# The inputs of the delta rule: one convolution, one projection and the sums of squares at other places in their queues

## What is computed

```python
q = silu(short_conv(hidden_states @ Wq, conv_q))      # 4 taps along the tokens
k = silu(short_conv(hidden_states @ Wk, conv_k))
v = silu(short_conv(hidden_states @ Wv, conv_v))
mix_inp = silu(short_conv(hidden_states @ Wmix, conv_mix))
q, k = silu(q), silu(k)
beta = sigmoid(hidden_states @ Wb)
gamma = sigmoid(hidden_states @ Wdec)
# delta_rule_chunkwise: q and k by their l2 norms (sums of squares by head of 64 channels),
#   attn = where(strict_lower, -(k_beta @ k^T), 0) in chunks of 32
# ema_rule: s = gamma * s + (1 - gamma) * v, one step per token
```

## Time and profile before

| | |
|---|---|
| time, median of 3 runs | 1435.75 us (1435.06 to 1437.74) |
| time of the profiled execution | 1436.34 us |
| its span in the trace | 1434.6 us |
| busy: PE | 1277.0 us (89%) |
| busy: DVE | 820.7 us (57%) |
| busy: ACT | 463.3 us (32%) |
| busy: POOL | 496.5 us (35%) |

### The profile page before, as it was taken

The page is one execution under the profiler, slowest core; times in us unless marked ns, Lnnn a source line. Parts: engine busy times, 40 slices in busy tenths (PEclk is TensorE's granted clock), DMA queues, the critical chain, the costliest instruction groups (busy, mean ns, idle before and its releaser), DMA issues. The chain is left out here.

```text
span 1434.6 us, 36334 instructions
## 1 busy us (share of the span) xinstructions
PE 1277.0 (89%) x12853; PEld 951.4 (66%) x12854; DVE 820.7 (57%) x1882; ACT 463.3 (32%) x1085; POOL 496.5 (35%) x709
## 2 busy tenths in 40 slices
PE   7999999899999999838888887298999999889997
PEld 5888888767776777614554555287888888746565
DVE  6788889533222222248888877457566666435443
ACT  1211222132222222226767774011222222123332
POOL 4344666415411111065666432223343434210000
PEclk9999999889999999968888997558999999779999
DMA  9999910113311211122444434612643334000001
GB/s 309 349 370 340 328 49 31 38 48 109 113 59 60 64 59 59 48 73 95 138 122 119 114 107 136 129 50 74 117 115 89 94 94 147 2 0 30 29 22 37
DMA packets 219962, 156.60 MB, mean 109 GB/s; under 512 B 111744, under 2 KB 201344, under 8 KB 219840
## 3 DMA queue, kind: packets, MB, share of 16 engines
q1 hardware_dynamic: 204288, 129.11, 30.7%
q0 software_dynamic: 9312, 25.44, 5.4%
q10 hardware_dynamic: 6240, 0.39, 0.3%
HBM read 64.47 MB, written 90.44 MB: 108 GB/s over the span
## 5 line engine op out<-in xcount | busy, mean ns | idle before, releaser
L945 PE MATMUL ps_sc<-w,a_qeo 128*128 x568 | 183.1, 466 | 0.0
L753 DVE TENSOR_TENSOR a_stm<-a_vpad,ps_sc 128x352 f32<-128x352 f32 x71 | 37.0, 521 | 177.2 <-ACT a_vpad L517 177.2
L945 PEld LDWEIGHTS ps_sc<-w,a_qeo 128*128 128x128 f32 x568 | 104.0, 193 | 46.5 <-issue 2.5
L423 POOL DMA_DIRECT2D x_slots<-a_stm x66 | 36.4, 551 | 226.1 <-issue 226.1
L1585 PE MATMUL d_pp<-d_xT,d_w_p 128*128 128x512 f32 x192 | 112.1, 732 | 1.1 <-ACT d_xT L1320 1.1
L1477 DVE SCALAR_TENSOR_TENSOR d_cout<-d_cin,d_taps,d_cout 128x512 f32<-128x512 f32 x144 | 106.1, 747 | 6.1 <-ACT d_cout L1338 2.7
L915 PE MATMUL ps_kv<-w,a_stm 128*128 x426 | 105.7, 384 | 1.2 <-DVE a_stm L746 1.1
L915 PEld LDWEIGHTS ps_kv<-w,a_stm 128*128 128x128 f32 x426 | 79.2, 190 | 30.1 <-issue 12.5
L2328 PE MATMUL g_pp<-g_xT,g_w_g 128*128 128x512 f32 x192 | 90.8, 613 | 8.3 <-ACT g_xT L2219 8.3
L1253 POOL DMA_INDIRECT got<-x_slots,d_idx x64 | 75.5, 1180 | 18.7 <-issue 16.1
L517 ACT ACTIVATE a_vpad<-ps_sc 128x352 f32<-128x352 f32 x71 | 33.0, 464 | 140.0 <-PE ps_sc L945 140.0
(11 more groups left out here) (273 smaller groups left out, 2834.4 us busy)
## 6 DMA issues: line engine op xcount, KB each, us to landing
x_slots<-a_zeros SPq DMA_DIRECT2D x32, 1024.0 KB, 11.0
rec<-d_kve SPq DMA_DIRECT2D x32, 384.0 KB, 2.9
u_kve<-rec SPq DMA_DIRECT2D x32, 384.0 KB, 3.9
a_qeo<-x_slots SPq DMA_DIRECT2D x71, 128.0 KB, 2.0
x_slots<-a_stm POOLq DMA_DIRECT2D x66, 128.0 KB, 2.1
rec<-d_act_out SPq DMA_DIRECT2D x32, 256.0 KB, 3.7
u_qkT<-rec SPq DMA_DIRECT2D x32, 256.0 KB, 3.5
w<-in_w SPq DMA_DIRECT2D x4, 1408.0 KB, 14.0
```

The lines of the kernel that those rows point to most:

```text
L753: dve.tensor_tensor(e_h[:, q, 0:HID], e_gate[:, q, :], ps_3[q], ALU.mult).then_inc(h_out, 1)
L945: mm = pe.matmul(ps, e_xT[:, q, k, :], w13[:, s, k, bass.ds(e_hidden, 1), :], start=(k == 0), stop=(k == KD - 1))
```

## The change

Three pieces change their places; the same instructions are executed.

On DVE, conv(2), the convolution of the first k block, stands ahead of the wait for `dec`, where it stood behind the scans. On PE, tokens(0) goes behind use(2). And the sums of squares, one piece behind use(7), are made in three: of the first tile of 128 tokens ahead of use(6), of the second ahead of use(7), of the last two where they stood. The first part waits for all the squares, as the whole did.

```diff
                 if here:
+                    conv(2)
+                if here:
                     dve.wait_ge(dec_done, u + 1)
                     dve.wait_ge(silu_done, 6 * u + 2)
                     dve.scalar_tensor_tensor(out=dec_t[:, :, :], in0=dec_t[:, :, :], scalar=1.0, in1=act_out[:, q, 4:6, :],
...
                            .then_inc(ema_done, 1)
-                if here:
-                    conv(2)
                 if i == NG:
                     rows(7, 11)
...
-                def sums():
+                def sums(of):
                     pe.wait_ge(sq_done, 4 * (v + 1))
                     pe.wait_ge(sm_out, v + 1)
-                    for j in range(GROUP):
+                    for j in of:
...
-                    mm.then_inc(sums_done, 1)
+                    if GROUP - 1 in of:
+                        mm.then_inc(sums_done, 1)
...
                 if tiles:
                     small_rows()
-                    tokens(0)
                 if here:
                     use(2)
                 if tiles:
+                    tokens(0)
                     tokens(1)
...
                 if tiles:
                     tokens(4)
+                    sums((0,))
                 if here:
                     use(6)
                 if tiles:
                     tokens(5)
+                    sums((1,))
                 if here:
                     use(7)
                 if tiles:
-                    sums()
+                    sums((2, 3))
```

## The result

The changed kernel takes 1446.02 us (median of seven, 1441.39 to 1453.68) where the kernel before took 1437.67 (median of seven, 1435.06 to 1439.70). The ratio, taken over all runs and not from the two medians (which give 1.0058), is 1.0064, with a 95% interval of 1.0039 to 1.0089. It is slower, by 0.64%, where 1429.7 us was forecast: outside the range, and on the side of rival C. In this document every ratio leaves out runs that fell in a slower state of the chip, which concerns four of the twelve of tokens_fill and two of the six of conv_fill_half (1451.19 and 1454.03 us), whose profile is of the first of these two.

A forecast was written before the change was run, and what follows sets the result against it. A ring through several engines, including DVE, was taken as the bound, with a PE and ACT ring 1.15 us behind. Pass gains 2.35 - 0.56 + 1.7 + 1.7 + 0.9 = 6.1 us, from 1435.75 to 1429.7; range 1424.5 to 1435.3.

The forecast's parts named there:

- rival C: New PE wait ahead of the first sums adds a low-clock stretch in passes 2 to 7, 1.78 us each: 1440.3; chance 0.07.
- a ring with DVE in it: Chain through several engines setting the 31.0 us period of pass 3; DVE's stretch from 709.10 to 718.6 is on it.
- a second of PE and ACT: Sums, use(8) to use(10) and ACT's silus, reaching conv(3)'s silu 1.15 us before DVE; claimed to limit the gain.
- Part (1): conv(2) on DVE ahead of the wait for dec: 2.29 us fit into 3.87 idle, DVE's ring stretch shrinks by 2.2.
- Part (2): tokens(0) behind use(2) on PE: use(2) starts no sooner, ring grows by 0.44 us a pass, bounds 0 and 0.9.
- Part (3): Sums in three parts, new PE wait for squares: use(8) starts 0.56 us later, dec 0.5 late, both including tokens(0)'s shift.
- the sum: Gains over the passes: 2.35 - 0.56 + 1.7 + 1.7 + 0.9 = 6.1 us, coming through whole to the kernel's time.
- The clock term: PE's low-clock stretch in use(8) to use(10): between 1.78 us won and 1.78 more lost per pass, taken as nought.
- Rival A: Clock held up in use(8) to use(10), passes 2 to 7 each gain 1.7: 12.8 us in all, 1423; chance 0.16.
- B: Gain mostly eaten, PE the bound of every inner pass: only 2.6 us remain, 1433.1, or 1434.8; chance 0.27.

The follow-up runs named there:

- tokens_fill: tokens(0) behind use(2), plus two idle 128x512 products in PE's wait ahead of use(2), against the kernel before: ratio 1.0031.
- conv_fill_half: conv(2) ahead of the wait for dec, idle products ahead of tokens(0), gram in half as many products, against the kernel before: ratio 0.9958.
- conv_only: Only conv(2) moved ahead of the wait for dec, against the kernel before: ratio 0.9917; the same measured again: 0.9965.
- tokens_only: Only tokens(0) moved behind use(2), against the kernel before: ratio 1.0065.
- after_fill: The whole change plus two idle wide products in each of PE's waits, ahead of use(2) and of the first sums, against the kernel before: ratio 0.9980.
- wait and cut alone: conv(2) ahead of dec's wait, plus only the new wait for squares: 0.9953; plus sums halved around use(8), no new wait: 0.9986; both against the kernel before.
- conv_gram: conv(2) ahead of the wait for dec, gram moved from behind tokens(2) to just ahead of the whole sums, against the kernel before: ratio 1.0048.
- conv_fill: conv(2) ahead of the wait for dec, plus two idle 128x512 products in PE's wait ahead of tokens(0), against the kernel before: ratio 0.9991.

## Why the prediction was wrong

**What bounds the kernel** was read rightly: a ring with DVE in it, and a second of PE and ACT 1.15 us behind. Part (1) alone bears both out: it gains, and of ACT's idle time before the silu of conv(3), 1.12 to 1.16 us in four passes before, 0.6 us is left in two passes of conv_only and none in the other four between the copies of passes 2 and 8.

**Part (1)** was right. By the prediction's own terms without those of (2) and (3), passes 2, 3, 6 and 7 give their 1.12 to 1.16, pass 4 nothing, passes 5 and 8 2.2 each, pass 1 0.9: 9.9 us. The stage of conv_only ends 9.7 us sooner; the two ratios give 11.9 and 5.0. That 9.9 and 9.7 agree is partly luck: pass 4, which was to give nothing, gave 3.9, and pass 5, which was to give 2.2, gave 0.7.

**Part (2)** was mis-sized by three: 0.44 us a pass, bounds 0 and 0.9, against 9.3 us by the ratio of tokens_only, some 1.3 a pass in seven. The wrong step is "use(2) starts no sooner, tokens(0) behind it costs its pitch". It counted tokens(0) at its price in full clock. In tokens_only it takes 1.92 us with tokens(1) in every second pass, the use(2) ahead of it 3.5 to 3.75, and ACT's queue waits for both. That ACT's copy of tokens(0) stands ahead of use(2)'s was seen; the 0.9 for it, which was the upper bound, was too small.

**Part (3)**, the hand-made order of time, was right as long as the clock is full: a wait forecast at 1.5 to 1.9 us is 1.43 and 1.47, and the fast pass 3 takes 29.58 us where 30.4 was forecast for the mean. (That mean doesn't follow from the sum, which wins 3.5 us in six passes and so gives 30.7.)

**The clock term is the step that failed.** "Its price per pass lies between all of the 1.78 won and 1.78 more lost; I take nought, since use(8) starts behind light work in either order." The group of twelve does behave so, from 5.40 to 8.33. But the bound was made from that group alone, as if only its products could be slow. Cut up and put behind a wait, the light work lowers the clock in use(6) or just behind it in three of the six passes, and use(6), tokens(5), use(7) and the sums pay too: 13.1 us more on the lines L1629 and L1576 in six passes. A slow pass costs 6.5 to 8.2 us more than a fast one, of which up to 1.4 are gaps in `gram`, not 1.78. Nought was taken for this term; over the six passes the kernel lost 15.0 us where the sum won 3.5, and after_fill, which takes the long stretches away, gives 12 us back.

**Rival C** named this mechanism with its place (use(6), use(7), the sums) and had 0.07. The argument against it, "low stretches replace each other rather than add up", is what the slow pass 2 refutes: one stretch of 13.6 us, 674.9 to 688.5, from use(6) into use(8) to use(10), where 3.4 us stood before. Its price was too low as well: it gave 1440.3, and 1446.0 was measured. Rival A, the clock held up, is what the fast passes show, at 29.6 us. B may have part of the truth: it said that PE would be the bound. The range was too narrow on the upper side since it left C out. With a second ring 1.15 us behind the first, and a term whose bounds were as wide as the whole gain, the chance of slower should have been near that of faster.

**Left open.** What decides between a slow and a fast pass of the same order of instructions; what the loss of (3) on top of (1) is made of beyond the clock, since wait and cut alone sum to 3 to 15 us of its 8 to 15, and gaps in `gram` take a part; and the cause of these gaps.

## What to carry to other kernels

Price a reordering on TensorE at both clock levels, and for all that stands between the new wait or the light work and the next wide products, not only for the group that is slow now. Small work that fills a wait for an operand is there for free: taken out of it, it cost 9.3 us here where 3.1 were put down. When one edit shortens a ring that another engine was the bound of, edits on TensorE have to be tried again together with it: here the third cost 5.5 us alone and 13.7 on top of the other two, and no combination of the three beat the first alone.

## What the hardware did that was not expected

- The clock falls behind light work even with PE busy without a break for the 6.8 us before (705.81 to 712.6 in conv_gram): 4.55 us of 128x8 products behind 1.42 us of `gram` end at 0.50, and the next twelve projections take 7.95 us instead of 5.40, in each pass.
- Two idle wide products in each of two waits of PE gave back 12 us (after_fill against after), with PE doing more work. In the five other kernels with filling nothing clear of noise was won.
- PE stops inside runs of small products, some 0.47 us after every three to five instructions, from the fortieth on, with nothing to wait for: 10.4 us in conv_fill, none in before. The stops in a row come only with the DMA engines busy to 0.22 or more in the 2 us from the start of `gram`; no run takes that traffic away, so whether it is a cause is not known. Where `gram` stood behind use(7) they did not come, with a share of 0.44 in conv_gram. A shortage in the supply of instructions would look like this, but no run here shows it. The Trainium skill ("Runtime: NRT & Kernel Launch", section "Instruction fetch mechanics") calls the cost of crossing from one block of instructions to the next "mostly hidden"; if it is the cause, it isn't hidden here.
- A stage that no edit touched, the delta rule, took between 333 and 347 us in nineteen of the twenty profiled executions, with its granted clock (0.90 and 0.85 at the two ends), and 360 at 0.83 in that of conv_fill_half. So a single span of this kernel tells less than its 0.2% between runs suggests; the stage's own end and the clock of its window tell more.
